# Three of four blocks of private activations move, in plain fp32, into the retrieval loop

## The chip, the cores and the metric

The kernel runs on one core of one Trainium2 chip. The metric is the device time of one execution in microseconds (us). Three runs of the kernel before gave 2097.33 us as their median (2095.89 to 2100.11). One execution was profiled; it took 2096.1 us, and its trace spans 2094.3 us from the first to the last instruction. All rows below are of that execution.

## What is computed

The reference is a stack of two layers on 2048 tokens of 256 features: attention with decay, a mixture of experts, a selective scan, and last a retrieval feed-forward; a layernorm follows each. The change is in the retrieval:

```python
h = silu(hidden_states @ W_up.T + b_up)          # 256 -> 1024
h = h @ W_down.T + b_down                        # 1024 -> 128, the "private activations"
q = h @ W_q.T                                    # 2 x 8 heads x 64
sim = einsum('pbthn,hkpn->pbthk', q, keys)       # 45 keys a head
scores, idx = top_k(sim, 8)
# best 8 of the 64 sums of each head -> indices into 2048 experts
z = silu(einsum('btd,bthkd->bthk', h, down_embed[indices]) * softmax(sc))
out = einsum('bthk,bthkd->btd', z, up_embed[indices])
```

## The kernel before, in words

The tokens are cut into 16 tiles of 128 (`TILES`) and 4 blocks of 512 (`BLK`, `NBLK`). `M.xT` holds the features of all tokens transposed, `h` the private activations of all tokens (128 features x 2048 tokens), `wk` the product of `W_q` and `keys`.

**`private_phase`** (from L1444) is a stage of its own. SyncE issues six loads (wu, bu, wd, bd, wq, keys) and then the retrieval's tables. TensorE waits for all six, forms `wk` (L1488) and then runs a loop over the 4 blocks. Each matrix is kept as a high part and a rest, both in fp32r, and a product is three fp32r matmuls: high by high, high by rest, rest by high. For a block these are 8 steps m (`UPT`) with 6 matmuls of 512 columns (L1500 to L1502), and 8 with 3 (L1510 to L1512). ScalarE applies Silu (L1563), VectorE splits the result into its two parts (L1544, L1546) and adds the bias (L1549). GpSimd splits the weights. A barrier of all engines ends the stage.

**`retrieval_phase`** (from L1573) then runs a software pipeline written out by hand, with semaphores and fixed orders of instructions on each engine. Its loop counter I goes from -3 to 16. In the pass I with all tiles alive, TensorE does, in this order: `gather(I)` (L1738, 192 small matmuls), the first quarter of `product(I-1)` (L1779), `select(I)` (L1751), then `fill_z(I+1)` (L1694) and `lower_z` (L1701) with the other quarters of `product(I-1)` and `turn(I+1)` (L1720, L1725) between them, `scatter(I)` (L1761), `scores(I+3)` (L1710) and `flip(I)` (L1771). VectorE does `marks(I)` (L1931, which `gather` needs; then L1922 and L1915), `normalize(I+1)`, `top_eights(I+2)` (L1975), `weigh(I)` (L1944 to L1949, needs `select`), `places_of(I+2)` (L1981, L1984), `cut(I)` (L1954 to L1966, needs ScalarE's `silu(I)`; `scatter` needs it), `bests` and `look_up(I+2)`, `add_out(I-1)`. ScalarE does the copies out of PSUM that lie between these (`pull` L1825, `copy_z` L1852, `copy_turned` L1844, `lift` L1831, `copy_scores` L1860, `copy_W` L1837), `silu(I)` (L1872) and, last in its pass, `soften(I+2)` (L1865, Exp). SyncE sends the tile's indices through DRAM and spreads them to all partitions, 2 MB (L1680). Passes -3 to -1 fill the pipeline; the first `gather` is in pass 0. A wait of the form `after(engine, name, count)` holds the engine until the semaphore has that count; what is behind it on the engine stays behind.

The PSUM banks `misc0` and `misc1` serve scores and z in turn; `ps_turned` serves `turn`. The buffers `W` and `masked` of the retrieval lie in the memory of `M.xT`, which nobody reads by then; `of_b` has two sets, used by alternate tiles.

## Time and profile before

| what | value |
|---|---|
| median of three runs | 2097.33 us |
| the profiled execution | 2096.1 us, span 2094.3 us |
| TensorE busy | 1773.3 us (85% of the span) |
| VectorE busy | 1275.2 us (61%) |
| ScalarE busy | 885.2 us (42%) |
| GpSimd busy | 487.4 us (23%) |
| mean granted TensorE clock | 0.939 of full |
| stage of the private activations | 1455.3 to 1553.0 us of the span |
| retrieval, pass -3 to the last sum | 1553.3 to 2077.3 us |

Busy shares are averages over stages with different limits, so the rows below are taken from the two stages that the change touches. A row of the timeline is: start, length, engine, line, operation, what it writes<-what it reads, how many instructions are merged; in brackets the idle time before it and what ended it. A merged row's length runs from the first start to the last end; matmuls are pipelined, so the spacing of starts is shorter than the length of one.

### The profile page before, as it was taken

To read this page: it belongs to the slowest core of one execution; us is meant where nothing else is said; L and a number is where in the kernel's file an instruction comes from. 1 tells how busy PE (TensorE), PEld (TensorE's weight loads), DVE (VectorE), ACT (ScalarE), POOL (GpSimd) and SP (SyncE) were. 2 spreads that over 40 slices of the span, in tenths; PEclk is the share of its full clock that TensorE was granted. 3 is DMA by queue.
4 is the path that set the end of the run, shared out by engine and by line. 5 is a ranking of instruction groups with operands and counts; after the bars stand their busy time and mean duration, and the time that the engine had idled before them with its cause. 6 is when DMAs were issued, how large, how long until landed. Compare 5 with 4: busy or idle time off the path is not lost. (4 is left out here: it accounts for less than half of the span.)

```text
span 2094.3 us, 44740 instructions
## 1 busy us (share of the span) xinstructions
PE 1773.3 (85%) x16696; PEld 1384.5 (66%) x16696; DVE 1275.2 (61%) x3096; ACT 885.2 (42%) x1542; POOL 487.4 (23%) x460
## 2 busy tenths in 40 slices
PE   6999999999997967999996466665977898989896
PEld 5888888888885756777773122222756787777775
DVE  0034344443445564644444799997369998989885
ACT  4533333333333332444444554443334655655652
POOL 1323342343326006600000466561200000000000
PEclk9999999999998976999998698888898999999998
DMA  2000000000002005223230000001103122122121
GB/s 85 18 2 23 23 23 10 13 23 23 23 10 93 0 9 176 91 86 88 82 99 23 0 0 1 0 0 50 66 0 123 43 83 84 43 83 84 43 83 42
DMA packets 55494, 96.81 MB, mean 46 GB/s; under 512 B 11424, under 2 KB 38176, under 8 KB 52776
## 3 DMA queue, kind: packets, MB, share of 16 engines
q1 hardware_dynamic: 55260, 94.94, 13.6%
q8 instruction: 84, 1.38, 0.3%
q14 instruction: 42, 0.34, 0.1%
q10 hardware_dynamic: 108, 0.15, 0.0%
HBM read 92.56 MB, written 2.51 MB: 45 GB/s over the span
## 5 line engine op out<-in xcount | busy, mean ns | idle before, releaser
L1351 POOL TENSOR_TENSOR sc_sb_bx<-sc_sb_dtx,sc_sb_bs 128x1024 f32<-128x1024 f32 x64 | 150.7, 2355 | 83.8 <-DVE sc_sb_h L1363 71.2
L1363 DVE TENSOR_TENSOR_SCAN sc_sb_h<-sc_ps_a,sc_sb_bx 128x512 f32<-128x512 f32 x128 | 150.5, 1209 | 20.6 <-ACT sc_ps_a L1341 20.6
L1852 ACT ACTIVATE re_sb_z<-re_ps_misc 128x512 bf16<-128x512 f32 x192 | 105.8, 594 | 124.0 <-PE re_ps_misc L1694 81.4
L544 POOL TENSOR_TENSOR g_sb_squares_sum<-g_sb_squares_sum,at_sb_qT 128x512 f32<-128x512 f32 x64 | 81.7, 1277 | 310.5 <-ACT at_sb_qT L475 310.5
L1067 DVE TENSOR_TENSOR mo_sb_gated<-mo_sb_hidden,mo_sb_gate 128x512 f32<-128x512 f32 x100 | 72.5, 725 | 131.2 <-ACT mo_sb_hidden L1037 130.7
L1037 ACT ACTIVATE mo_sb_hidden<-mo_ps_h,mo_sb_b 128x512 f32<-128x512 f32 x100 | 68.8, 688 | 162.3 <-PE mo_ps_h L995 162.0
L1284 PE MATMUL sc_ps_y<-sc_sb_hc,all_sb_ident 128*128 128x512 f32 x256 | 126.7, 626 | 0.0
L1779 PE MATMUL re_ps_out<-re_sb_up,all_sb_xT 128*128 128x256 f32 x512 | 121.9, 383 | 0.9 <-ACT all_sb_xT L1837 0.9
L506 DVE COPY at_sb_state<-at_ps_state_sum 128x128 f32<-128x128 f32 x64 | 18.6, 290 | 168.9 <-PE at_ps_state_sum L420 168.9
L1738 PE MATMUL re_ps_wheel<-re_sb_is_b,re_sb_z 128*32 128x128 bf16 x3072 | 76.4, 261 | 36.1 <-issue 30.2
L515 DVE SCALAR_TENSOR_TENSOR g_sb_gated<-at_ps_out,at_sb_nw,g_sb_gated 128x512 f32 x64 | 48.1, 751 | 94.3 <-ACT at_sb_qT L475 94.3
L1779 PEld LDWEIGHTS re_ps_out<-re_sb_up,all_sb_xT 128*128 128x128 f32 x512 | 95.0, 190 | 15.1 <-ACT all_sb_xT L1837 1.1
L1738 PEld LDWEIGHTS re_ps_wheel<-re_sb_is_b,re_sb_z 128*32 128x32 bf16 x3072 | 72.7, 192 | 41.3 <-issue 41.2
L475 ACT ACTIVATE at_sb_qT<-at_ps_out 128x512 f32<-128x512 f32 x64 | 38.2, 597 | 127.5 <-PE at_ps_out L436 127.5
L1275 PE MATMUL sc_ps_c<-sc_sb_bc_parts,sc_sb_state_rows 96*128 96x512 bf16 x64 | 27.2, 425 | 76.4 <-DVE sc_sb_hc L1371 76.4
L1329 ACT ACTIVATE sc_sb_bs<-sc_ps_b 128x512 f32<-128x512 f32 x64 | 38.1, 596 | 121.1 <-PE sc_ps_b L1275 121.1
L1005 PE MATMUL mo_ps_acc<-mo_sb_gatedH,mo_sb_w2H 128*128 128x512 f32 x200 | 81.4, 407 | 8.3 <-DVE mo_sb_gatedL L1059 8.3
L993 PE MATMUL mo_ps_h<-mo_sb_xH,mo_sb_w1H 128*128 x200 | 80.5, 402 | 6.0 <-DVE all_sb_xT_part L1054 6.0
L500 DVE TENSOR_TENSOR at_sb_weights<-at_ps_score,at_sb_tbl 128x512 f32<-128x512 f32 x128 | 81.9, 682 | 5.1 <-PE at_ps_score L407 5.1
L1230 POOL TENSOR_TENSOR sc_sb_dtx<-sc_sb_dt,all_sb_xT x8 | 12.7, 1582 | 307.3 <-DVE sc_sb_dt L1221 307.3
L1275 PEld LDWEIGHTS sc_ps_c<-sc_sb_bc_parts,sc_sb_state_rows 96*128 96x128 bf16 x64 | 6.2, 97 | 117.7 <-DVE sc_sb_hc L1371 116.7
L1341 ACT ACTIVATE sc_ps_a<-sc_sb_dt,sc_sb_decay 128x512 f32<-128x512 f32 x128 | 82.9, 685 | 1.8 <-DVE sc_sb_h L1363 1.8
(258 smaller groups left out, 5048.7 us busy)
## 6 DMA issues: line engine op xcount, KB each, us to landing
re_sb_b_all<-re_b SPq DMA_DIRECT2D x16, 2048.0 KB, 8.2
mo_sb_gate<-mo_gates SPq DMA_DIRECT2D x36, 256.0 KB, 3.1
mo_sb_w<-in_w_dram SPq DMA_DIRECT2D x10, 640.0 KB, 9.5
at_sb_w<-in_qkv_w_dram SPq DMA_DIRECT2D x18, 256.0 KB, 3.0
mo_sb_gate<-mo_gates SPq DMA_DIRECT2D x20, 192.0 KB, 2.7
mo_sb_gate<-mo_gates SPq DMA_DIRECT2D x16, 224.0 KB, 3.1
at_sb_tbl<-in_decay_dram SPq DMA_DIRECT2D x18, 193.5 KB, 2.3
mo_sb_gate<-mo_gates SPq DMA_DIRECT2D x20, 160.0 KB, 2.6
```

The source lines that it names most:

```text
L500: nc.vector.tensor_tensor(weights[:, h, :].rearrange("p (t q) -> p t q", t=CHUNKS), ps_score[h][:, :].rearrange("p (t q) -> p t q", t=CHUNKS),
L544: nc.gpsimd.tensor_tensor(part, part, qT[n][:, :], ALU.add).then_inc(summed, 1)
L993: nc.tensor.matmul(ps_h[f % NP][:, :], w1H[:, c, fs], xH[xs], start=(c == 0), stop=False)
L1005: nc.tensor.matmul(acc[d][:, :], w2H[:, g, of], gatedH[g % NH][:, :], start=(g == 0), stop=False)
L1067: nc.vector.tensor_tensor(gated[f % 2][:, :], hidden[f % 2][:, :], gate[f % NG][:, :], ALU.mult).then_inc(gated_ready, 1)
L1284: last = nc.tensor.matmul(ps_y[:, d * BLK:(d + 1) * BLK], M.ident[:, :], hc[g % HCS][:, d, :], start=(n == 0), stop=(n == STATES - 1))
L1341: nc.scalar.activation(a[g % 2][d][:, :], dt[:, d, tokens(g)], ACT.Exp, scale=decay[:, d, g % STATES:g % STATES + 1]).then_inc(a_ready, 1)
L1351: nc.gpsimd.tensor_tensor(bx[g % BXS][:, :, :], dtx[:, :, tokens(g)], bs[g % BSS][:, :].unsqueeze(1).broadcast_to([P, KD, BLK]), ALU.mult) ...
L1363: nc.vector.tensor_tensor_scan(h[g % 2][:, d, :], a[g % 2][d][:, :], bx[g % BXS][:, d, :], 0.0, ALU.mult, ALU.add).then_inc(scanned, 1)
L1738: last = nc.tensor.matmul(wheel[g * 2 * ROWS:(g + 1) * 2 * ROWS, j * P:(j + 1) * P], z[:, n, :, :, token].rearrange("p a r -> p (a r)"), i ...
L1779: last = nc.tensor.matmul(ps_out[:, 0:DM], W[:, a, :], up[:, a, :], start=(a == 0), stop=(a == ROWS - 1))
L1852: nc.scalar.activation(z[:, n, :, 4 * j:4 * j + 4, :], misc[j % 2][:, :].rearrange("p (r a t) -> p a r t", r=4, a=2), ACT.Copy).then_inc(S ...
```

## The change

`private_phase` keeps one block, the first (tokens 0 to 511), done in plain fp32: 2 matmuls a step for `wu`, 1 for `wd`, no splitting, nothing on VectorE or GpSimd. ScalarE also adds the bias. `wq` and `keys` are loaded first and waited for on their own. The other three blocks are 12 pieces of a quarter block of hidden units each (2 of the 8 steps m). Piece p belongs to block 1 + p // 4. In the retrieval's loop TensorE does `rise_product(I+3)` last in a pass and `private_product(I+2)` after `gather(I)`; ScalarE does `rise_up(I+3)` between `copy_W` and `soften`; VectorE does `keep_h(I+2)` between `top_eights` and `weigh`, which adds the piece into `h`. So pieces 0 to 11 go up in passes -3 to 8 and down in passes -2 to 9. New waits on `h_kept`, `up_ready`, `h_used` guard the shared banks. As `M.xT` is still read, `W` and `masked` get memory of their own, and `of_b` has one set in place of two, with a wait for the scatter of the tile before in `marks`.

```diff
 @block.tensor   (private_phase)
-                pe.wait_ge(loaded, 6 * 16)
+                pe.wait_ge(keys_loaded, 2 * 16)
...
-                with pe.Fori(0, NBLK) as i:
-                    pe.wait_ge(x_low, i + 1)
-                    for m in range(UPT + LAG):
...
+                pe.wait_ge(up_loaded, 4 * 16)
+                for m in range(UPT + LAG):
+                    if m < UPT:
+                        if m >= NB:
+                            pe.wait_ge(up_ready, m - NB + 1)
+                        for c in range(KD):
+                            last = nc.tensor.matmul(ps_up[m % NB][:, :], wu[:, c, m * P:(m + 1) * P],
+                                                    M.xT[:, c, 0:BLK], start=(c == 0), stop=(c == KD - 1))
+                        last.then_inc(up_product, 1)
+                    if m >= LAG:
+                        g = m - LAG
+                        pe.wait_ge(up_ready, g + 1)
+                        nc.tensor.matmul(ps_h[:, :], wd[:, g, :], rise[g % NB][:, :], start=(g == 0),
+                                         stop=(g == UPT - 1)).then_inc(h_product, 1)
...
+                act.wait_ge(h_product, UPT)
+                nc.scalar.activation(h[:, 0:BLK], ps_h[:, :], ACT.Identity, bias=bd[:, 0:1])
...
-        of_b = [[s.sb(f"of_b{n}{c}", [P, HALF_TWIN // 2, GRID, 2], BF16) for c in range(2)] for n in range(2)]
+        of_b = [s.sb(f"of_b{c}", [P, HALF_TWIN // 2, GRID, 2], BF16) for c in range(2)]
...
                 def scores(T, m):
+                    after(pe, "h_kept", T // 4 * 4)
...
                 def turn(T):
                     after(pe, "turned_ready", T * 2)
+                    after(pe, "h_kept", min(T + 2, PIECES))
...
+                def rise_product(piece, I):
+                    block = 1 + piece // 4
+                    for n in range(2):
+                        m = piece % 4 * 2 + n
+                        after(pe, "sim_ready", (I + 3) * 2 + n + 1)
+                        for c in range(KD):
+                            last = nc.tensor.matmul(misc[n][:, :], wu[:, c, m * P:(m + 1) * P],
+                                                    M.xT[:, c, block * BLK:(block + 1) * BLK],
+                                                    start=(c == 0), stop=(c == KD - 1))
+                        last.then_inc(S["up_product"], 1)
+
+                def private_product(piece, I):
+                    after(pe, "up_ready", 2 * (piece + 1))
+                    after(pe, "turned_ready", (I + 1) * 2)
+                    after(pe, "h_kept", piece)
+                    for n in range(2):
+                        last = nc.tensor.matmul(ps_turned[:, :], wd[:, piece % 4 * 2 + n, :], rise[n][:, :],
+                                                start=(n == 0), stop=(n == 1))
+                    last.then_inc(S["h_used"], 1)
...
                         for q in range(QUARTERS):
                             gather(I, q)
+                    if 0 <= I + 2 < PIECES:
+                        private_product(I + 2, I)
                     if live(I - 1):
                         product(I - 1, 0)
...
                             flip(I, q)
+                    if 0 <= I + 3 < PIECES:
+                        rise_product(I + 3, I)
...
+                def rise_up(piece):
+                    after(act, "h_used", piece)
+                    for n in range(2):
+                        after(act, "up_product", 2 * piece + n + 1)
+                        m = piece % 4 * 2 + n
+                        nc.scalar.activation(rise[n][:, :], misc[n][:, :], ACT.Silu, bias=bu[:, m:m + 1]
+                                             ).then_inc(S["up_ready"], 1)
...
                             copy_W(I, q)
+                    if 0 <= I + 3 < PIECES:
+                        rise_up(I + 3)
                     if live(I + 2):
                         soften(I + 2)
...
-                    after(dve, "scattered", (T - 1) * QUARTERS)
+                    after(dve, "scattered", T * QUARTERS)
                     of_bs(T, 0)
...
+                def keep_h(piece):
+                    after(dve, "h_used", piece + 1)
+                    after(dve, "h_kept", piece)
+                    of = h[:, (1 + piece // 4) * BLK:(2 + piece // 4) * BLK]
+                    if piece % 4 == 0:
+                        last = nc.vector.tensor_scalar(of, ps_turned[:, :], bd[:, 0:1], None, ALU.add)
+                    else:
+                        last = nc.vector.tensor_tensor(of, ps_turned[:, :], of, ALU.add)
+                    last.then_inc(S["h_kept"], 1)
...
                         top_eights(I + 2)
+                    if 0 <= I + 2 < PIECES:
+                        keep_h(I + 2)
                     if live(I):
                         weigh(I)
```

## Rows read from the trace of the kernel before

**Rows 1.** Stage windows: busy us of each engine, granted clock, DMA share, GB/s.
```profile
1455.00:1475.00 20.00, 8.36 (x35) 8.06 (x36) 4.63 (x4) 3.96 (x5) 8.35 (x20) 0.55 0.96 291
1831.00:1862.00 31.00, 28.28 (x548) 24.17 (x548) 28.55 (x110) 17.96 (x34) 0.00 (x0) 1.00 0.18 70
```

**Rows 2.** Timeline of TensorE, one pass of the retrieval (I = 3) and the next start.
```profile
1675.40 4.45 PE L1738 MATMUL re_ps_wheel<-re_sb_is_b,re_sb_z 128*32 128x128 bf16 x192 [1.71 <-issue]
...
1681.70 2.09 PE L1751 MATMUL re_ps_wheel<-re_sb_twin,re_sb_pulled 128*64 128x64 f32 x64
...
1701.81 1.91 PE L1771 MATMUL re_ps_wheel<-all_sb_ident,re_sb_lifted 128*128 128x128 f32 x16
1705.44 0.78 PE L1738 MATMUL re_ps_wheel<-re_sb_is_b,re_sb_z 128*32 128x128 bf16 x25 [1.72 <-issue]
```

**Rows 3.** Timeline of VectorE in the same pass.
```profile
1674.55 2.74 DVE L1931 TENSOR_SCALAR re_sb_is_b<-re_sb_b_all,re_sb_own 128x2048 bf16<-128x2048 bf16 x4
...
1684.55 1.27 DVE L1944 TENSOR_TENSOR all_sb_xT<-re_ps_wheel,re_sb_of_a 128x512 f32<-128x512 f32 x2
...
1692.21 0.23 DVE L1954 TENSOR_TENSOR re_sb_c_rest<-re_sb_c_whole,re_sb_c_parts 128x64 f32<-128x64 f32 x1 [0.62 <-ACT re_sb_c_parts L1874]
```

**Rows 4.** Timeline of ScalarE at the end of the same pass.
```profile
1704.59 1.28 ACT L1865 ACT_TABLE_LOAD   x1
1705.88 0.27 ACT L1865 ACTIVATE re_sb_soft<-re_sb_soft 128x64 f32<-128x64 f32 x1
```

**Rows 5.** Timeline of TensorE: the private stage's start, its end, and the fill.
```profile
1466.64 7.06 PE L1488 MATMUL pv_ps_k<-pv_sb_keys,pv_sb_wq 64*128 64x45 f32 x32 [12.25 <-DMA pv_sb_keys<-in_keys_dram]
1473.62 0.79 PE L1500 MATMUL pv_ps_up<-pv_sb_xH,pv_sb_wuH 128*128 x1
...
1477.49 0.40 PE L1500 MATMUL pv_ps_up<-pv_sb_xH,pv_sb_wuH 128*128 x1
1477.73 0.39 PE L1501 MATMUL pv_ps_up<-all_sb_xT_part,pv_sb_wuH 128*128 x1
...
1553.27 2.88 PE L1710 MATMUL re_ps_misc<-re_sb_wk,re_sb_h 128*128 128x360 f32 x8 [1.32 <-PEq L1474]
1561.70 3.78 PE L1694 MATMUL re_ps_misc<-re_sb_h,re_sb_down 128*128 128x128 f32 x16 [5.55 <-ACT re_sb_sim L1860]
...
1583.78 4.88 PE L1738 MATMUL re_ps_wheel<-re_sb_is_b,re_sb_z 128*32 128x128 bf16 x192 [5.54 <-DVE re_sb_is_b L1931]
```

**Rows 6.** Timeline; two source lines (ns min/median/max, first and last start); a DMA issue.
```profile
1435.15 5.32 PE L1284 MATMUL sc_ps_y<-sc_sb_hc,all_sb_ident 128*128 128x512 f32 x12
L1563 ACT ACTIVATE pv_sb_up<-pv_ps_up,pv_sb_bu x32: 681/688/689, 1477.9 to 1548.8; 128x512 f32<-128x512 f32 x32
L1549 DVE TENSOR_SCALAR re_sb_h<-pv_ps_h,pv_sb_bd x4: 751/751/752, 1495.3 to 1552.2; 128x512 f32 x4
pv_sb_wu<-in_w_up_dram SPq DMA_DIRECT2D x1, 1024.0 KB, 4.9
```

**Rows 7.** Timeline of VectorE in the fill, and clock windows there (columns of Rows 1).
```profile
1556.48 1.74 DVE L1975 MAX8 re_sb_top<-re_sb_sim 128x8 f32<-128x45 f32 x16
...
1582.89 2.74 DVE L1931 TENSOR_SCALAR re_sb_is_b<-re_sb_b_all,re_sb_own 128x2048 bf16<-128x2048 bf16 x4
1562.00:1565.00 3.00, 3.00 (x15) 3.00 (x15) 2.93 (x26) 2.15 (x4) 0.00 (x0) 0.50 0.01 3
```

**Rows 8.** Timelines: VectorE's marks of passes 1 and 14, TensorE's gather of pass 6.
```profile
1611.92 2.74 DVE L1931 TENSOR_SCALAR re_sb_is_b<-re_sb_b_all,re_sb_own 128x2048 bf16<-128x2048 bf16 x4
...
1768.54 2.26 PE L1738 MATMUL re_ps_wheel<-re_sb_is_b,re_sb_z 128*32 128x128 bf16 x92 [1.49 <-issue]
1772.04 2.50 PE L1738 MATMUL re_ps_wheel<-re_sb_is_b,re_sb_z 128*32 128x128 bf16 x100 [1.24 <-issue]
...
2018.62 2.74 DVE L1931 TENSOR_SCALAR re_sb_is_b<-re_sb_b_all,re_sb_own 128x2048 bf16<-128x2048 bf16 x4
```

More of the change, by code:

```diff
@@ L1459, in private_phase @@
         NB, LAG = 4, 2
-        up = [s.sb(f"up{n}", [P, BLK]) for n in range(NB)]
-        upH = [s.sb(f"upH{n}", [P, BLK], FP32R) for n in range(NB)]
-        upL = [s.sb(f"upL{n}", [P, BLK], FP32R) for n in range(NB)]
+        rise = [s.sb(f"rise{n}", [P, BLK]) for n in range(NB)]
         ps_up = [s.ps(f"up{n}") for n in range(NB)]
@@ L1568, in _ @@
                                          ps_k[n][:, 0:RHEADS * KEYS], ACT.Copy)
+                act.wait_ge(up_loaded, 4 * 16)
+                for m in range(UPT):
+                    act.wait_ge(up_product, m + 1)
+                    if m >= NB:
+                        act.wait_ge(h_product, m - NB + 1)
+                    nc.scalar.activation(rise[m % NB][:, :], ps_up[m % NB][:, :], ACT.Silu,
+                                         bias=bu[:, m:m + 1]).then_inc(up_ready, 1)
+                act.wait_ge(h_product, UPT)
+                nc.scalar.activation(h[:, 0:BLK], ps_h[:, :], ACT.Identity, bias=bd[:, 0:1])
 def retrieval_phase(nc, M, D):
@@ L1598, in load_tables @@
                 sp.dma_start(to, of).then_inc(tables_loaded, 16)
-        private_phase(nc, M, D, h, wk, load_tables)
+        wu = s.sb("wu", [P, KD, CROSS])
+        wd = s.sb("wd", [P, UPT, PRIV])
+        bu = s.sb("bu", [P, UPT])
+        bd = s.sb("bd", [P, 1])
+        private_phase(nc, M, D, h, wk, wu, wd, bu, bd, load_tables)
+        rise = [s.sb(f"rise{n}", [P, BLK]) for n in range(2)]
+        PIECES = (NBLK - 1) * UPT // 2
         sim = s.sb("sim", [P, 2 * RHEADS, KEYS])
```

108 lines of the change are left out of this document (17 added, 91 removed).

## The prediction

> **What bounds the kernel now.** I read the windows by stage first, then the timelines of TensorE and VectorE over one pass of the retrieval, then both ends of the private stage, then the fill between the two.
>
> The private stage runs from the first load at 1455.3 us to 1553.3, where the first scores start [rows 5]. The first eleven microseconds go to loads: TensorE waits for the last of six, `keys`, until 1466.64. Then 7.06 us go to `wk` at about half clock (0.55 in that window, rows 1), and the four blocks run from 1473.62. At full clock an fp32r matmul of 512 columns starts 0.24 us after the one before (1477.49 and 1477.73, rows 5). A block has 8 x 6 + 8 x 3 = 72 of them, and TensorE sets the pace: (1553.3 - 1473.6) / 4 = 19.9 us a block, waits at its ends and the barrier included.
>
> In the retrieval TensorE and VectorE bound the pass together. In pass 3, `gather` starts at 1675.40 and again at 1705.44: 30.04 us [rows 2]. TensorE's only long rest is ahead of `gather`: `flip` ends at 1701.81 + 1.91 = 1703.72, then 1.72 us idle. It waits there for VectorE: the marks start at 1674.55 and the first quarter takes a quarter of 2.74 us, then `gather` goes [rows 3]. VectorE is busy nearly throughout and has one wait, 0.62 us for ScalarE's Silu of z at 1692.21, which comes through TensorE's `turn`. So the loop is closed this way: marks, gather, select, turn, Silu, `cut`, `look_up`, marks. TensorE's own work is 28.3 us of the pass. Other passes look the same; marks of pass 1 start at 1611.92 and of pass 14 at 2018.62 [rows 8], so the mean pass is 406.7 / 13 = 31.3 us. The excess over 30.0 sits in some passes in gaps inside `gather`, as the 1.24 us at 1772.04 [rows 8]. TensorE is busy 28.3 of 31 us at full clock [rows 1].
>
> **Unit prices.** A plain fp32 matmul appears as two instructions in the trace: `product` has 256 calls, `scores` 32 and the scores of one tile already count as four. Twelve instructions of 512 columns take 5.32 us [rows 6]; less the 0.59 us of the last one that is 0.43 us each, so 0.86 us a call. `rise_product` is 4 calls, 3.4 us; `private_product` 2 calls, 1.7 us; a piece 5.1 us, twelve pieces 62 us. Three blocks before cost 59.7 us. On TensorE alone the change saves nothing: what it can gain is the place. `rise_up` is two Silus of 0.69 us, `keep_h` one VectorE step of 0.75 us [rows 6].
>
> **The private stage after.** Removed: everything of three blocks, and the start that waits for all loads. `wq` and `keys` now go first. They have not been seen in that place. `wu`, twice as large, landed 4.9 us after its issue in first place [rows 6], so 1461 is my value for `keys`; the other end is 1466.6, as now. `wk` then takes 7.1 us, to 1468, and the other four loads are in by 1466.6. One block is 16 + 8 = 24 calls, 24 x 0.86 = 20.6 us at full clock. Now the clock became full some 10.8 us after TensorE started (1466.64 to 1477.5, rows 5); if that repeats, full clock comes at 1471.8 and the 3.6 us before are worth 1.8, so the block ends at 1490.6. ScalarE's bias (0.2 + 0.7) and the same 0.3 us to the first scores give 1491.8. Against 1553.3 that is **-61.5 us**; with `keys` late, -56.
>
> **The fill (passes -3 to -1).** Here VectorE bounds: busy from 1556.48 without a gap to the marks of tile 0 at 1582.89 [rows 7], and TensorE waits 5.55 and 5.54 us [rows 5]. In the same coordinates: scores of tile 0 (the first half of the row at 1553.27) end at 1554.7, `rise_product(0)` runs behind them to 1558.1, its Silus end at 1559.0, `private_product(0)` at 1560.8. `top_eights(0)` ends at 1556.48 + 1.74 = 1558.2, and behind it VectorE now waits in `keep_h(0)` for that product: 2.8 us, and 0.75 for the step itself, so everything behind on VectorE is 3.5 us late. The scores of tile 1, whose copy waits for VectorE's `places_of`, come as late, and with them `rise_product(1)`, which stands ahead of `fill_z(0)` on TensorE. At full clock TensorE's chain of rise 1, Silu, down 1, z of tile 0, scores 2, rise 2 ends before VectorE is there, and the fill costs 3.5 + 0.75 = 4.3 us. But TensorE idles before it, and at just this place the clock now falls to half (0.50 at 1562 to 1565, after the rest of 5.55 us; rows 5, 7). At half clock `rise_product(1)` takes 6.8, down 1 3.4, and the chain (an estimate: about 14 us for z and scores 2, from 3.78 us for each of z's two fills at half clock and the copies between, and 3.4 for rise 2) ends 11 to 12 us later than `gather(0)` now starts. The rest ahead of it is shorter than now (some 3 us), so I take the middle, **+8 us**, range 4 to 12.
>
> A page speaks against this place: the Trainium skill (ScalarE: Activation LUTs, What ACT_TABLE_LOAD costs) prices a switch of table set at 2.66 us, a load of 1.28 and a drain of 1.38. The trace agrees on the load (1.28 us) but the Exp starts 0.01 us behind it [rows 4]. The new order Silu, Exp, Silu, Exp in the fill adds two switches, 2.6 us by the row and 5.3 by the page, both on ScalarE beside VectorE's 26 us.
>
> **The loop.** Pass 0 has no `product`, so TensorE has room: `keep_h` 0.75 and what of rise 3 sticks out past the marks, 3.4 - 1.8 = 1.6 us: +1.5 to 2.4, taken as **+2**. In passes 1 to 8 `private_product` stands between `gather` and `select`, and `rise_product` between `flip` and the next `gather`. TensorE's path from one `gather` to the next becomes 28.3 + 5.1 = 33.4 us. VectorE's: c_parts came 16.8 us after `gather` and comes 1.7 later, 18.5; from there to the next marks 12.4 and to `gather` 0.85 as now: 31.8 us. TensorE sets the pass: 33.4 against 30.0, +3.4 us. That is 5.1 less the 1.72 us of rest, which goes. Eight passes: **+27 us**. Pass 9 has only the down part: +1.7 on the path through `turn`: **+2 us**. Covered, and with what: `keep_h` (0.75) by VectorE's wait for `select`: `select` ends at 8.4 us after `gather` now (1681.70 + 2.09) and at 10.1 then, while VectorE, its marks 0.85 + 1.6 us ahead of `gather`, is there at -2.45 + 10.0 + 0.75 = 8.3; `rise_up` (1.4) by ScalarE, 18 us busy of 31, and it needs no new table, since `silu(I)` left Silu in place and only copies follow. `soften` behind it moves to 2.5 us after `gather` starts, so the first `pull` is about 1.3 us late; quarters come every 1.1 us and a copy takes 0.6, so the fourth is on time. If that cover failed it would cost up to 1.3 us a pass, 12 us in all. Queued behind `rise_product` is `gather`; behind `keep_h`, `weigh`. The single `of_b`: its wait for the scatter of the tile before is reached some 34 us after the `gather` of that tile's pass; the scatter is over before `flip`, which starts at 26.4 now (1701.81) and 28.1 then; nothing, and 6 us in hand. SyncE's queue is unchanged. Long passes: the gaps inside `gather` may stay or go, as the 2 MB spread now falls earlier against it; 0 to -9 us over eight passes (their excess over 30.0 in total), and I take 0.
>
> **Sum.** -61.5 + 8 + 2 + 27 + 2 = -22.5. On the profiled execution's own 2096.1 us that gives 2073.6; the median of the runs lies 1.2 above it. I say **2074.5 us**.
>
> **The rivals.**
> - *The gaps go too.* With the rest before `gather` gone TensorE never pauses, the excess of the long passes (9 us) vanishes and the fill stays at full clock (-4): 2061. For: some long passes have gaps marked as issue, not as waits. Against: nothing shows that they depend on VectorE.
> - *The cover fails in part.* `keys` land late (+5.5), the fill at half clock (+4) and the late `pull` (up to +12, half of it taken, +6): 2090. For: ScalarE's order is now pull behind soften behind Silu behind the rise. Against: the arithmetic above.
> - *The loop takes the additions in full (slower).* Mechanism: rise, Silu, down, keep and marks turn out to be one chain, so that the 1.7 us of rest is a wait for something behind the rise and is not filled. Then each of passes 0 to 8 costs 5.1 + 0.75 = 5.9 us, 53 in all, pass 9 2.5, the fill 12: +67.5 against -61.5, so 2103. It decides from 5.2 us a pass (12 + 9 x 5.2 + 2.5 = 61.3). For: every piece adds a semaphore round over three engines. Against: VectorE's marks need nothing of pass I's rise.
> - *No net change.* The same chain in part, just at that 5.2 us a pass: 2097.
>
> **How the numbers follow.** Forecast (2067 to 2082) 0.56; gaps go (2057 to 2067) 0.16; cover fails (2082 to 2093) 0.16; no net change 0.04; slower 0.08. About 0.2% (4 us) is what a measurement of this kernel can tell from no change. Faster: 0.56 + 0.16 + 0.16 = 0.88; same 0.04; slower 0.08. The range leaves out a tenth at either side: 2061 to 2089.
>
> **What would show it.** Right: the first scores some 61 us earlier; marks of pass 0 some 26 to 38 us behind them plus 3; a spacing of `gather` of 33.4 us in passes 1 to 8 and 30 to 31 from pass 10; no idle time ahead of `gather` in passes 1 to 8; VectorE's waits for `select` of 1 to 2 us. Wrong: idle time ahead of `gather` beside a longer pass (slower rival), a `pull` that holds up `select` (cover), or half clock in passes 1 to 8.

## The result

The changed kernel takes 2064.93 us (median of 4 runs, 2062.97 to 2070.13) against 2098.01 us for the kernel before (4 runs, 2095.89 to 2100.11). The ratio is 0.9843, 95% interval 0.9826 to 0.9861: 33 us faster. A second set of 5 runs of the same kernel gave 0.9849 [0.9832, 0.9865]. The time is below the forecast of 2074.5 us and inside the range of 2061 to 2089 us. It does not lie in the forecast's own band (2067 to 2082) but in that of the rival "the gaps go too" (2057 to 2067, chance 0.16). The profiled execution took 2062.97 us (span 2061.2) beside 2096.1 (span 2094.3) before.

I cut both executions at the same events, and the pieces add up to the whole difference of 33.1 us. "First scores" is the start of `scores` of tile 0, "gather(n)" the first gather of pass n.

| stretch | before | after | difference | forecast |
|---|---|---|---|---|
| start to first scores | 1553.27 | 1492.54 | -60.7 | -61.5 |
| first scores to gather(0) | 30.51 | 34.55 | +4.0 | +8 |
| pass 0 | 28.99 | 31.42 | +2.4 | +2 |
| passes 1 to 8 | 250.03 | 271.58 | +21.6 | +27 |
| pass 9 | 32.71 | 31.79 | -0.9 | +2 |
| passes 10 to 15 and the end | | | +0.5 | 0 |

The stretch up to the first scores, and then the fill, on the timeline of TensorE of the kernel after (they answer to [rows 5]; start, duration, engine, line, operation, output and inputs, count, in brackets the idle time before and what ended it):

```profile
1460.80 7.05 PE L1476 MATMUL pv_ps_k<-pv_sb_keys,pv_sb_wq 64*128 64x45 f32 x32 [6.72 <-DMA pv_sb_keys<-in_keys_dram]
1467.78 2.07 PE L1485 MATMUL pv_ps_up<-all_sb_xT,re_sb_wu 128*128 128x512 f32 x2
...
1492.54 1.45 PE L1656 MATMUL re_ps_misc<-re_sb_wk,re_sb_h 128*128 128x360 f32 x4 [1.02 <-PEq L1462]
1493.95 3.70 PE L1738 MATMUL re_ps_misc<-all_sb_xT,re_sb_wu 128*128 128x512 f32 x8
1498.42 1.98 PE L1749 MATMUL re_ps_turned<-re_sb_rise,re_sb_wd 128*128 128x512 f32 x4 [0.78 <-ACT re_sb_rise L1855]
...
1504.56 5.26 PE L1738 MATMUL re_ps_misc<-all_sb_xT,re_sb_wu 128*128 128x512 f32 x8 [2.94 <-ACT re_sb_sim L1833]
...
1527.09 1.16 PE L1685 MATMUL re_ps_wheel<-re_sb_is_b,re_sb_z 128*32 128x128 bf16 x41 [0.81 <-DVE re_sb_is_b L1915]
```

`keys` are there at 1460.80 instead of 1466.64, `wk` takes as long as before, the block starts at 1467.78. In the fill the timeline of VectorE shows the new wait in `keep_h(0)`, and the marks of tile 0, which answer to [rows 7]:

```profile
1500.45 0.75 DVE L2038 TENSOR_SCALAR re_sb_h<-re_ps_turned,re_sb_bd 128x512 f32<-128x512 f32 x1 [2.96 <-PE re_ps_turned L1749]
...
1526.20 2.74 DVE L1915 TENSOR_SCALAR re_sb_is_b<-re_sb_b_all,re_sb_own 128x2048 bf16<-128x2048 bf16 x4
```

`gather(0)` waits 0.81 us for those marks: VectorE, not TensorE, sets the end of the fill.

One pass of the loop on TensorE (pass 2, answering to [rows 2]). The two added pieces are L1749 and L1738:

```profile
1592.27 4.57 PE L1685 MATMUL re_ps_wheel<-re_sb_is_b,re_sb_z 128*32 128x128 bf16 x192
1596.77 1.98 PE L1749 MATMUL re_ps_turned<-re_sb_rise,re_sb_wd 128*128 128x512 f32 x4
...
1600.41 2.09 PE L1698 MATMUL re_ps_wheel<-re_sb_twin,re_sb_pulled 128*64 128x64 f32 x64
...
1620.47 1.91 PE L1718 MATMUL re_ps_wheel<-all_sb_ident,re_sb_lifted 128*128 128x128 f32 x16
1622.22 3.60 PE L1738 MATMUL re_ps_misc<-all_sb_xT,re_sb_wu 128*128 128x512 f32 x8
1625.75 0.50 PE L1685 MATMUL re_ps_wheel<-re_sb_is_b,re_sb_z 128*32 128x128 bf16 x11
```

From gather to gather it is 33.48 us, and no idle time stands in brackets ahead of the second gather, where [rows 2] had 1.72 us. `rise_product` ends where `gather` starts. The window of that pass, with the columns of [rows 1]: TensorE is busy 32.30 of 33 us at full clock, where it was 28.28 of 31.

```profile
1592.00:1625.00 33.00, 32.30 (x560) 26.05 (x560) 29.02 (x110) 19.31 (x35) 0.00 (x0) 1.00 0.18 66
```

VectorE in the same pass on its timeline (answering to [rows 3]), and after it ScalarE on its own:

```profile
1599.76 0.73 DVE L2038 TENSOR_SCALAR re_sb_h<-re_ps_turned,re_sb_bd 128x512 f32<-128x512 f32 x1
1601.68 0.69 DVE L1928 TENSOR_TENSOR re_sb_masked<-re_ps_wheel,re_sb_of_a 128x512 f32<-128x512 f32 x1 [1.19 <-PE re_ps_wheel L1698]
...
1610.91 0.22 DVE L1938 TENSOR_TENSOR re_sb_c_rest<-re_sb_c_whole,re_sb_c_parts 128x64 f32<-128x64 f32 x1 [1.91 <-ACT re_sb_c_parts L1847]
```

```profile
1596.89 0.60 ACT L1798 ACTIVATE re_sb_pulled<-re_ps_wheel 128x512 f32<-128x512 f32 x1 [0.41 <-PE re_ps_wheel L1685]
```

VectorE now has 1.19 and 1.91 us to spare (0.62 in [rows 3]), and the fourth `pull` ends at 1597.5, well before `select` at 1600.41: both covers of the forecast hold.

One pass is not like the others. In pass 5 the matmuls of `gather` stop for 3.07 us, marked as issue, and the next gather is at 1729.45, 36.65 us after this one (1692.80):

```profile
1692.80 4.47 PE L1685 MATMUL re_ps_wheel<-re_sb_is_b,re_sb_z 128*32 128x128 bf16 x190
1700.35 0.28 PE L1685 MATMUL re_ps_wheel<-re_sb_is_b,re_sb_z 128*32 128x128 bf16 x2 [3.07 <-issue]
...
1729.45 1.80 PE L1685 MATMUL re_ps_wheel<-re_sb_is_b,re_sb_z 128*32 128x128 bf16 x68
```

I call the time of passes 1 to 8 above eight undisturbed ones the *excess*: before 250.03 - 8 x 30.04 = 9.7 us, after 271.58 - 8 x 33.4 = 4.4 us. This is where the time went better than forecast, beside the fill, and most of the experiments are about it. Each excess below is that of one profiled execution. The base is a regular pass near the shortest of its kernel; what the other passes without a visible gap take above it (mostly under 0.6 us each) counts in the excess too.

### The profile page after: what moved, and what is told of

Its sections match the earlier page's. It is cut to its first block and busy times, and to the rows that moved or that the text cites. A ratio compares the mean times of both kernels' runs of the same rounds, so it can differ in the third digit from the quotient of the medians.

```text
span 2061.2 us, 44242 instructions
## 1 busy us (share of the span) xinstructions
PE 1782.8 (86%) x16600; PEld 1361.4 (66%) x16600; DVE 1240.5 (60%) x3036; ACT 879.3 (43%) x1538; POOL 475.1 (23%) x428
## 3 DMA queue, kind: packets, MB, share of 16 engines
q8 instruction: 85, 1.39, 0.3%
## 5 line engine op out<-in xcount | busy, mean ns | idle before, releaser
L1726 PE MATMUL re_ps_out<-re_sb_up,re_sb_W 128*128 128x256 f32 x512 | 121.0, 381 | 0.9 <-ACT re_sb_W L1810 0.9
L1726 PEld LDWEIGHTS re_ps_out<-re_sb_up,re_sb_W 128*128 128x128 f32 x512 | 95.7, 190 | 18.6 <-issue 4.5
```

Source lines behind the costliest of these rows:

```text
L1726: last = nc.tensor.matmul(ps_out[:, 0:DM], W[:, a, :], up[:, a, :], start=(a == 0), stop=(a == ROWS - 1))
```

## The experiments

Each ratio is against the kernel before in the same set of runs (medians 2096.4 to 2098.5 us).

**Is it the place, or the cheaper arithmetic?** The loop of the kernel before, with the private stage doing all four blocks in plain fp32 and `wq` and `keys` loaded first:

```diff
-                                nc.tensor.matmul(ps_up[m % NB][:, :], wuH[:, c, of], xH[xs], start=(c == 0), stop=False)
-                                nc.tensor.matmul(ps_up[m % NB][:, :], wuH[:, c, of], xL[xs], start=False, stop=False)
-                                last = nc.tensor.matmul(ps_up[m % NB][:, :], wuL[:, c, of], xH[xs],
-                                                        start=False, stop=(c == KD - 1))
...
+                            last = nc.tensor.matmul(ps_up[g % NB][:, :], wu[:, c, m * P:(m + 1) * P],
+                                                    M.xT[:, c, i * BLK:(i + 1) * BLK], start=(c == 0), stop=(c == KD - 1))
```

> The kernel before with one part of the change: the private stage as in the change (wq and keys loaded first, plain fp32, no splitting), but for all four blocks, and the retrieval's loop untouched. Theory of place: the gain of the change comes from where the three blocks are done, not from how. The stage then starts its first block 6 us earlier (1467.8 for 1473.6), a block takes 8 x 2.57 = 20.6 us for 19.9, the end 0.9: first scores at about 1467.8 + 1.8 + 82.4 + 1.2 = 1553 us of the span, as before; the time within 3 us of before. Rival, the cheaper stage: the stage without splits and with earlier loads carries a third or more of the 33 us; then 11 us or more faster than before.

Measured: 2094.78 us (10 runs), ratio 0.9988 [0.9978, 0.9997]. The timeline of TensorE:

```profile
1463.05 7.05 PE L1480 MATMUL pv_ps_k<-pv_sb_keys,pv_sb_wq 64*128 64x45 f32 x32 [6.90 <-DMA pv_sb_keys<-in_keys_dram]
...
1556.50 1.97 PE L1661 MATMUL re_ps_misc<-re_sb_wk,re_sb_h 128*128 128x360 f32 x5 [1.02 <-PEq L1466]
```

From `wk` to the first scores it is 93.4 us, against 86.6 in [rows 5]: the plain work is 6.8 us longer. It gets 5.3 us of that back by its start: `wk` begins 6.0 us after the first load is issued, where it was 11.3. From the first load to the first scores the stage takes 99.4 us against 98.0. By the medians the kernel is 2.5 us faster, within the 3 us expected. So a stage of its own costs nearly the same in either arithmetic, and the 33 us come of the place. The opposite half, the old arithmetic in the new place, was not run.

**What does the rest ahead of gather take in?** The kernel before with unused fp32 matmuls behind `flip` in passes 1 to 8, two (1.7 us a pass) and four (3.4 us); the edit with four:

```diff
+                    if 1 <= I <= 8:
+                        after(pe, "sim_ready", (I + 3) * 2 + 2)
+                        for n in range(4):
+                            nc.tensor.matmul(misc[n % 2][:, :], down[:, 0:P], down[:, P:P + BLK], start=True, stop=True)
```

> The kernel before with two plain fp32 matmuls of 512 columns (1.7 us of TensorE, on the tables, into the banks that rise_product uses) behind flip in passes 1 to 8; they are used by nobody. Theory: the 1.7 us of rest ahead of gather is a wait for VectorE's marks and takes them in full: 0 us in all (0 to +2), gather to gather still 30 to 33 us. Rival, one chain: the rest moves behind them, 8 x 1.7 = +14 us.

> The same with four such matmuls, 3.4 us, the whole of a rise_product. Theory: 1.7 us of each is taken by the rest, 1.7 sticks out: 8 x 1.7 = +14 us (+11 to +16), no rest left ahead of gather; less if the gaps inside gather get rarer once the 2 MB spread starts ahead of it. Rival, one chain: +27 us.

Measured: with two 2093.74 us, ratio 0.9986 [0.9975, 0.9996]; with four 2114.94 us, 1.0085 [1.0068, 1.0102]. The timeline of TensorE with two, one pass:

```profile
1706.24 1.88 PE L1822 MATMUL re_ps_misc<-re_sb_down 128*128 128x512 f32 x4
1708.20 1.03 PE L1738 MATMUL re_ps_wheel<-re_sb_is_b,re_sb_z 128*32 128x128 bf16 x36
```

Passes 1 to 8 take 249.9 us as before (250.0): the rest of 1.72 us is filled free of charge. The next 1.7 us have their full price: 264.5, or 14.6 us more for 8 x 1.7 = 13.8. By the medians the four cost 17.7 us over the kernel before, more than the 11 to 16 expected. The profiled execution with four was the shortest of its runs and the one with two among their longest, so the step between these two is less certain than its decimals. It is still the forecast's step "5.1 less the 1.72 us of rest", and it rules out the slower rival, in which the rest can't be filled. But the rest is gone here too and the excess stayed: 9.6 with two, 10.3 with four (over an undisturbed pass of 31.77). So taking the rest away isn't enough to lower the excess, as the rival "the gaps go too" had it.

**Do the gaps belong to the 2 MB spread?** The spread of the slot numbers over the partitions (`b_all`) cut from 2 MB to 16 KB from tile 1 on, in the kernel before and in the kernel after. The output is then not that of these tokens, since the marks compare old slot numbers; every instruction of the engines stays.

```diff
-                    sp.dma_start(b_all[:, :, :].rearrange("p t k -> p (t k)"), b_dram[T % 2].partition_broadcast(P)
-                                 ).then_inc(S["b_spread"], 16)
+                    if T:
+                        sp.dma_start(b_all[:, 0, 0:SLOTS], b_dram[T % 2][0:SLOTS].partition_broadcast(P)
+                                     ).then_inc(S["b_spread"], 16)
...
```

> The kernel before with the spread of the indices cut from 2 MB to 16 KB from tile 1 on (so the marks and the output of tiles 1 to 15 are not those of their tokens; all instructions but that DMA are the same). Theory: the gaps inside gather and select, marked issue, come when TensorE's instruction stream has to be refilled while the 2 MB spread fills the DMA engines. Without it they go, every pass 1 to 13 is 30.0 us, and the kernel is 13 to 17 us faster. Rival, the gaps have nothing to do with the DMAs: the same passes (2, 5, 6, 8, 9, 12) stay 1 to 3 us long, within 3 us of before.

> The changed kernel with the spread cut to 16 KB from tile 1 on (marks and output of tiles 1 to 15 are then not those of their tokens). Cutting it took 9 us off the kernel before, and the gaps in select went while part of those in gather stayed. Theory: the changed kernel has already got rid of some of what the spread costs, since the spread now starts 1.7 us ahead of gather and runs beside rise_product; so less is left, 3 to 6 us. Rival, the lower cost of passes 1 to 8 has another cause: again 9 us.

Measured: on the kernel before 2088.22 us, ratio 0.9959 [0.9945, 0.9973], 9 us less; on the kernel after 2060.02 us, 0.9821 [0.9805, 0.9838], 6 us less than its second set of runs (2066.03). Passes 1 to 8 fall to 245.1 (excess 4.8) and to 268.8 (excess 1.6). The expectation for the kernel before, 13 to 17 us, was too high. In the kernel after, the gap of pass 5 shrinks from 3.07 to 0.42 us at the same matmul, the last two of 192; in the kernel before, gaps inside gather remain up to 1.35 us (the 1.61 in the rows below is the rest ahead of it). The timelines of TensorE, first of the kernel after with the small spread, then of the kernel before with it:

```profile
1691.78 4.50 PE L1689 MATMUL re_ps_wheel<-re_sb_is_b,re_sb_z 128*32 128x128 bf16 x190
1696.70 0.28 PE L1689 MATMUL re_ps_wheel<-re_sb_is_b,re_sb_z 128*32 128x128 bf16 x2 [0.42 <-issue]
```

```profile
1860.09 2.47 PE L1742 MATMUL re_ps_wheel<-re_sb_is_b,re_sb_z 128*32 128x128 bf16 x103 [1.61 <-issue]
1863.92 2.23 PE L1742 MATMUL re_ps_wheel<-re_sb_is_b,re_sb_z 128*32 128x128 bf16 x89 [1.35 <-issue]
```

So the transfer makes the long gaps long, but something of TensorE's own instruction supply is there without it.

**Can the spread be made gentler?** The kernel after with the spread in four parts of 512 KB, each issued when the one before has landed:

```diff
+                    for n in range(4):
+                        of = slice(n * P * SLOTS // 4, (n + 1) * P * SLOTS // 4)
+                        sp.dma_start(b_all[:, :, :].rearrange("p t k -> p (t k)")[:, of],
+                                     b_dram[T % 2][of].partition_broadcast(P)).then_inc(S["b_spread"], 16)
+                        sp.wait_ge(S["b_spread"], (T * 4 + n + 1) * 16)
```

> The changed kernel with the 2 MB spread issued as four parts of 512 KB, each after the one before has landed; all of it is done, over some 14 us of the pass in place of 10, and it is needed only 20 us later. Theory: the long gaps on TensorE (3.07 us in pass 5, and 1 to 1.6 in passes 11 and 12) come when a refill of its instruction stream has to pass a long spread; shorter bursts shorten them: 3 to 6 us faster than the changed kernel. Rival, the gaps are the refill's own or the spread's total: within 2 us of it.

Measured: 2066.12 us, ratio 0.9848: no gain, where 3 to 6 us were expected. Passes 1 to 8 take 272.1 us; pass 5 is 35.4 us long with its gap shortened to 1.79, and pass 3, regular before, is 35.8 with one of 2.13. So in these passes nothing is gained. But the total hides two changes that cancel. Beside the second set's profiled execution the fill is 3.8 us longer (38.35 for 34.57), because the four parts in series bring the indices of tile 0 later and `gather(0)` waits 4.65 us for the marks, and passes 10 to the end are 2.8 us shorter (197.3 for 200.1). Whether smaller parts help where the fill doesn't pay for them stays open.

**The kernel after once more, and without the wait in keep_h(0).** The second set of runs of the unchanged kernel after, and one edit that puts `keep_h(0)` behind VectorE's `places_of` of its pass:

```diff
-                    if 0 <= I + 2 < PIECES:
+                    if 0 <= I + 2 < PIECES and I > -2:
                         keep_h(I + 2)
...
+                    if I == -2:
+                        keep_h(I + 2)
```

> The changed kernel once more, unchanged, as the yardstick on this chip for the three beside it: 2063 to 2070 us.

> The changed kernel with keep_h(0) of pass -2 moved behind places_of(0) on VectorE; all else as it is. Theory: the fill costs 4 us because VectorE waits 2.96 us in keep_h(0) for private_product(0), ahead of places_of(0), on which the scores of tile 1 and rise 1 hang; with the step behind places_of that wait is covered, TensorE does not idle and rise 1 runs at full clock (3.6 us for 5.26): marks of tile 0 some 3 us earlier, 3 us faster than the changed kernel. Rival, TensorE's chain through rise 1, down 1, z and rise 2 bounds the fill: 0 to 1 us.

Measured: unchanged 2066.03 us (2063.16 to 2069.54), edited 2064.46 us (2058.8 to 2065.81), ratios 0.9849 and 0.983. The fill behaves as calculated: from the first scores to the marks of tile 0 it is 30.61 us instead of 33.66. On TensorE the rest ahead of the second rise is gone and the rise has its full speed:

```profile
1504.31 3.70 PE L1738 MATMUL re_ps_misc<-all_sb_xT,re_sb_wu 128*128 128x512 f32 x8
...
1700.64 0.28 PE L1685 MATMUL re_ps_wheel<-re_sb_is_b,re_sb_z 128*32 128x128 bf16 x2 [2.94 <-issue]
```

But passes 1 to 8 take 274.4 us instead of 271.6: pass 5 is again long (38.4 us, the last row), and pass 3 as well (35.1, with a gap of 1.58). The gap of pass 5 is no longer than before; its pass is 1.7 us longer because the granted clock fell behind the gap, and `private_product` took 3.41 us for 1.98:

```profile
1700.86 3.41 PE L1749 MATMUL re_ps_turned<-re_sb_rise,re_sb_wd 128*128 128x512 f32 x4
```

```profile
1701.00:1705.00 4.00, 4.00 (x7) 1.99 (x8) 0.69 (x1) 0.56 (x1) 0.00 (x0) 0.57 0.02 4
```

In the kernel after the clock stayed at 1.00 from 1700.5 to 1705 us, behind a gap of 3.07. The repeated run of the unchanged kernel has its one long pass at the same place, pass 5 with 36.4 us and a gap of 2.77. In all of them the gap of pass 5 stands behind the 190th matmul of `gather`. The one of pass 3 is new here, and stands at the same matmul (behind the 169th) as in the kernel with the spread in parts. So an edit on VectorE leaves the places as they are and changes which of them show a gap.

**TensorE's whole added work, on the kernel before.** The run with four matmuls behind `flip`, and two more (1.7 us) between gather and the first select:

```diff
+                    if 1 <= I <= 8:
+                        after(pe, "turned_ready", (I + 1) * 2)
+                        for n in range(2):
+                            nc.tensor.matmul(ps_turned[:, :], down[:, 0:P], down[:, P:P + BLK], start=True, stop=True)
```

> The kernel before with TensorE's whole added work of passes 1 to 8 and nothing else of the change: four unused plain fp32 matmuls (3.4 us) behind flip and two (1.7 us) between gather and the first select. Compare with the run that has the first four alone: 2114.9, passes 1 to 8 264.5 us, of which 10.5 are long passes. Theory (the gaps lie in what TensorE does beside the 2 MB spread, and the change moves select and the following product out from beside it): the passes take 33.4 us plus less than 5 us of excess in all, 267 to 272 us, and the time is 2118 to 2123. Rival (the excess stays whatever stands there; the change loses it for another reason): 8 x 33.4 + 10 = 277 us and 2128 to 2130.

Measured: 2121.22 us (4 runs, 2119.66 to 2125.78), ratio 1.0114 [1.0097, 1.0131]. The time is the theory's, but the profiled execution, the longest of the four, is the rival's: passes 1 to 8 take 277.3 us, six of them 33.3 to 34.0, two of them 38.19 and 37.51. It is 4.6 us above the median. Part of that may lie ahead of the retrieval, where this kernel equals the one before: `wk` starts 3.6 us later than in that one's profiled execution. The timeline of TensorE in the first of these:

```profile
1684.02 4.33 PE L1738 MATMUL re_ps_wheel<-re_sb_is_b,re_sb_z 128*32 128x128 bf16 x184
1691.25 0.39 PE L1738 MATMUL re_ps_wheel<-re_sb_is_b,re_sb_z 128*32 128x128 bf16 x8 [2.89 <-issue]
```

Two things follow. The undisturbed pass of 33.4 us is TensorE's added work and nothing else of the change (no ScalarE or VectorE step of it is in this kernel). And "the work moves out from beside the spread" didn't by itself bring the smaller excess: the same placing of work has 10.1 us of it in this execution. Some 3 us of that are the clock: behind the gaps of 2.89 and 2.52 us it fell to 0.58 and 0.57 (means of 4 us). The three shorter executions were not profiled, so this is one case, not a mean.

**Only the place in TensorE's instruction stream.** The kernel after with 96, then with 32, semaphore increments on TensorE ahead of its wait for `keys`; no work is changed:

```diff
+                for n in range(32):
+                    pe.sem_inc(pad, 1)
                 pe.wait_ge(keys_loaded, 2 * 16)
```

> The kernel after with 96 semaphore increments on TensorE ahead of its wait for keys, where it has nothing to do: no work is changed, every later instruction of TensorE lies 96 places further on in its stream. Theory (the one long pass, the fifth, with its 2.8 to 3.1 us gap at 7.5 us in gather, is where a refill of TensorE's instructions meets the spread): the long pass is another one, or its gap another size, and the time is 2062 to 2070. Rival (the gap belongs to pass 5's own data or addresses): pass 5 is again 36.4 to 36.7 us long and every other one 33.4 to 33.8.

> The kernel after with 32 instead of 96 semaphore increments on TensorE ahead of its wait for keys. The 96 took 15.6 us there (0.163 us each) where only some 6.7 were idle and so held up wk by themselves; 32 take 5.2 us and fit into the 6.72 us of waiting: first scores again at 1492.4 to 1492.8 us, and only the place of every later instruction in TensorE's stream is changed. Theory (the gaps are where TensorE's instructions are fetched beside the 2 MB spread, so they go by the place in the stream): other passes than the fifth are long, by 1 to 5 us each, and the time is 2063 to 2075. Rival (the three long passes with the 96 come of the later start): with the start as before only the fifth pass is long, at 36.4 to 36.7 us, and the time is 2063 to 2069.

Measured: with 96 2080.08 us, ratio 0.9918 [0.9904, 0.9933]; with 32 2070.91 us, 0.9866 [0.9849, 0.9882]. The 96 were a badly chosen size: TensorE was idle for 15.6 us ahead of `wk`, which started at 1471.91, and the first scores came at 1502.60, 10.1 us late by the increments' own cost. That is most of the miss against the expected 2062 to 2070; the other part is more gaps. The 32 hide as intended. The timeline of TensorE with 32:

```profile
1461.66 7.05 PE L1478 MATMUL pv_ps_k<-pv_sb_keys,pv_sb_wq 64*128 64x45 f32 x32 [7.76 <-DMA pv_sb_keys<-in_keys_dram]
...
1492.88 1.45 PE L1658 MATMUL re_ps_misc<-re_sb_wk,re_sb_h 128*128 128x360 f32 x4 [1.02 <-PEq L1462]
...
1701.43 0.65 PE L1687 MATMUL re_ps_wheel<-re_sb_is_b,re_sb_z 128*32 128x128 bf16 x18 [3.07 <-issue]
...
1773.48 1.02 PE L1751 MATMUL re_ps_turned<-re_sb_rise,re_sb_wd 128*128 128x512 f32 x2 [1.73 <-issue]
```

The first scores are 0.3 us from where they were, and yet the kernel is 5 us slower than in its second set of runs. Pass 5 is still the longest, now 38.55 us (1.7 of it again half clock behind the gap, 0.57 from 1702 to 1706) and with its gap at another matmul (18 before the end of gather, not 2); pass 7 is long as well, with a gap inside `private_product`, and of the later passes the 12th takes 35.42 us (33.32 in the kernel after). The excess of passes 1 to 8 is 7.8 us. With 96 the long passes are 2, 4 and 9 (37.21, 34.99, 36.39 us) and pass 5 is regular at 33.46. That pass 5's own data or addresses make the gap is ruled out: with 96 increments it has none, and with 32 it has it elsewhere. The expectation that with 32 pass 5 would be regular was wrong.

The shift itself can be read off. With 32 increments the gap of pass 5 comes 16 matmuls earlier (174 for 190), those of pass 12 16 earlier (89 for 105, 216 for 232), and the one of pass 11 15 earlier (130 for 145); with 96 the last is 47 earlier (98). Each of these matmuls has a weight load of its own, so 16 of them are 32 instructions and 48 are 96. The possible places of a gap are fixed in TensorE's stream; which of them show one is not, as the edit on VectorE showed.

The profile page of the kernel after has, in its part on DMA queues, TensorE's own instruction queue:

```profile
q8 instruction: 85, 1.39, 0.3%
```

85 packets with 1.39 MB are 16 KB each, and three of them fall into the 20 us from 1685 to 1705, in which pass 5 has its gap. The Trainium skill (Runtime: NRT & Kernel Launch, Instruction fetch mechanics) says that an engine's instructions come in blocks of 16 KiB by a DMA queue of its own, and that this fetch is mostly hidden. The trace agrees on the size. On the second point it agrees for most of the packets, but some of the fetches show. The DMA view of the kernel after for the gap of pass 5 alone, from 1697.2 to 1700.4 us, has one such packet among those of the spread (queue q1):

```profile
q1 hardware_dynamic: 67, 0.85, 63.8%
q8 instruction: 1, 0.02, 1.9%
```

In the trace this packet starts at 1697.94 and ends at 1698.90, and the matmuls go on at 1700.35, 1.45 us later. It is the same in the other kernels. From the first to the last `gather` the fourteen kept traces have 98 gaps of more than 0.35 us marked issue that are not at the first matmul of a gather. Every one of them ends 1.2 to 1.6 us after a packet of this queue has ended. The 100 idle times of that size ahead of the first matmul of a gather are different: there the last packet had ended at least 2.9 us before. So those, the rests for the marks, are not of this kind. The 98 are waits for the next block of instructions. They run from 0.4 to 3.1 us and get shorter when the 2 MB transfer is cut. What stays open is which block comes late: that I could not work out.

**A version with both small things mended.** The kernel after with `keep_h(0)` later, the loads of `wu`, `bu`, `wd`, `bd` ahead of `wq` and `keys`, and `wk` formed inside the first block, at full clock:

```diff
+                    if m == 5:
+                        pe.wait_ge(keys_loaded, 2 * 16)
+                        for n in range(2 * RHEADS):
+                            last = nc.tensor.matmul(ps_k[n // RHEADS][:, n % RHEADS * KEYS:(n % RHEADS + 1) * KEYS],
+                                                    wq[:, n, :], keys[:, n, :], start=True, stop=True)
+                        last.then_inc(k_product, 1)
...
```

> The kernel after with two edits: keep_h(0) behind places_of of its pass (alone: 2064.5, the fill 3.05 us shorter), and the loads of wu, bu, wd and bd ahead of wq and keys, with wk formed between the tiles 4 and 5 of the first block's up products, at full clock. Theory: wk takes some 4 us there instead of 7.05 at half clock, the blocks start when wu has landed (about 1460.8), and the half clock falls on up products instead: first scores 0 to 3 us earlier than 1492.5, time 2059 to 2065. Rival: the wait for keys (up to 1466.6) now falls inside the block, or the full clock comes later after it: no gain or a loss of up to 3 us.

Measured: 2062.44 us (2059.36 to 2063.04), ratio 0.9833 [0.9819, 0.9848]. The timeline of TensorE, then windows (busy of each engine, then the granted clock, third number from the right):

```profile
1462.29 7.34 PE L1486 MATMUL pv_ps_up<-all_sb_xT,re_sb_wu 128*128 128x512 f32 x12 [8.77 <-DMA re_sb_bd<-in_b_down_dram]
...
1475.58 3.77 PE L1479 MATMUL pv_ps_k<-pv_sb_keys,pv_sb_wq 64*128 64x45 f32 x32
1479.27 3.23 PE L1486 MATMUL pv_ps_up<-all_sb_xT,re_sb_wu 128*128 128x512 f32 x4
1482.31 1.51 PE L1492 MATMUL pv_ps_h<-pv_sb_rise,re_sb_wd 128*128 128x512 f32 x2
```

```profile
1475.00:1479.00 4.00, 4.00 (x33) 3.42 (x31) 0.00 (x0) 0.51 (x1) 0.00 (x0) 1.00 0.00 1
1479.00:1482.00 3.00, 3.00 (x8) 1.46 (x7) 0.00 (x0) 0.00 (x0) 0.00 (x0) 0.64 0.00 0
```

`wk` takes 3.77 instead of 7.05 us, as expected. But behind its 32 matmuls of 45 columns the granted clock falls, though TensorE was busy throughout, and the next six instructions take 4.4 us (1479.27 to 1483.65) instead of 2.6. The first scores come at 1491.70, 0.8 us earlier than in the kernel after, though TensorE started 1.5 us later: 2.3 us were gained, of some 3. The fill is again 3.05 us shorter. Of these 4 us passes 1 to 8 take back most (passes 3 and 5 with 35.71 and 38.23 us, excess 8.1), 1.7 us of it by half clock behind the gap of pass 5 (0.57 from 1698 to 1702). It is the fastest version of all that compute the whole, 2.5 to 3.6 us below the two sets of runs of the changed kernel, but the intervals overlap.

## Why the forecast was right, and where it was off

*The private stage, -61.5: right, -60.7.* `keys` were there at 1460.80 (value taken: 1461), `wk` kept its 7.05 us, the first up product was at 1467.78 (1468). The late end of the range (1466.6) didn't come. The 0.7 us too few are the clock: the first twelve instructions of the block took 8.29 us where 5.3 would be full speed, 3.0 us lost against the 1.8 taken.

*The fill, +8: over-sized; it was +4.0.* The wait in `keep_h(0)` was 2.96 us (2.8) and the step 0.75. The step that failed is the middle taken between full and half clock for TensorE's chain. The granted clock did fall, and `rise_product(1)` took 5.26 us, between 3.6 and 6.8; but the matmuls behind it ran at full clock again (down 1 in 1.98 us), so the chain stayed hidden behind VectorE and only the full-clock figure of 4.3 counted. The windows of the kernel after:

```profile
1501.00:1505.00 4.00, 1.06 (x4) 0.49 (x3) 3.97 (x37) 0.83 (x2) 0.00 (x0) 0.92 0.00 0
1505.00:1510.00 5.00, 4.82 (x8) 1.64 (x7) 4.83 (x30) 0.83 (x2) 0.00 (x0) 0.73 0.00 0
```

The rest ahead of that rise was 2.94 us instead of 5.55 [rows 5], as foreseen, and that shorter rest should have moved the value towards the lower end, not to the middle. The extra switches of table cost what [rows 4] showed. On ScalarE's timeline of the kernel after the load takes 1.28 us and Exp follows 0.01 us after it:

```profile
1510.57 1.28 ACT L1838 ACT_TABLE_LOAD   x1
1511.86 0.26 ACT L1838 ACTIVATE re_sb_soft<-re_sb_soft 128x64 f32<-128x64 f32 x1
```

The Trainium skill (ScalarE: Activation LUTs, What ACT_TABLE_LOAD costs) adds to each switch a drain of 1.38 us. It does not show here.

*Pass 0, +2: right, +2.4.*

*Passes 1 to 8, +27: the mechanism right, the size 5.4 too large.* The undisturbed pass is 33.4 us (33.40 to 33.76 in seven of eight), no idle time is ahead of gather, VectorE waits for `select` 1 to 2 us, and `keep_h`, `rise_up` and the later `pull` are covered. The fillers show the same by themselves: 1.7 us free, the rest at full price. The step that failed is "0 to -9 us ..., and I take 0": the excess fell from 9.7 to 4.4 us, 5.3 less, by two things.

About 2.1 us is the clock. The prediction put the excess down to gaps inside gather and took the passes to be at full clock, by the window of pass 8 alone. But in passes 2 and 5 of the kernel before the granted clock fell at the start of `gather`, and `gather` took 5.41 and 5.63 us where [rows 2] had 4.45. The timeline of TensorE, and the window of the first:

```profile
1643.07 5.41 PE L1738 MATMUL re_ps_wheel<-re_sb_is_b,re_sb_z 128*32 128x128 bf16 x192 [1.80 <-issue]
...
1735.65 5.63 PE L1738 MATMUL re_ps_wheel<-re_sb_is_b,re_sb_z 128*32 128x128 bf16 x192 [2.00 <-issue]
```

```profile
1643.00:1648.00 5.00, 4.81 (x180) 4.59 (x184) 5.00 (x6) 2.52 (x5) 0.00 (x0) 0.66 0.46 164
```

Both stand behind the rest that the change fills, so in this part the rival "the gaps go too" was right that TensorE's rest costs. It did not cost it every time: behind rests of 1.83 and 1.80 us in passes 1 and 7 the clock stayed at 1.00. In passes 1 to 8 of the kernel after, and of its second profiled execution, it is 1.00 throughout. There was luck in that too: behind gaps of about 3 us it fell in the kernels with `keep_h(0)` later, with 32 increments and with `wk` inside, and cost 1.7 us each.

Of the other 3.2 us, 1.3 are waits for instructions: those over 0.35 us come to 4.4 us in passes 1 to 8 before and to 3.1 after. The remaining 1.9 us I can't assign, and why the waits got fewer is open. The reason that the forecast gave, that the spread now lies earlier, is not borne out by the kernel before with all six matmuls: it has the same placing and, in the one execution profiled, 10.1 us of excess. Over the profiled executions of six kernels or sets of runs with the change's loop and the full, undivided spread the excess is 4.4, 4.6, 5.9, 7.2, 7.8 and 8.1 us, mean 6.3; over five with the loop of before, with or without fillers, it is 7.8, 9.6, 9.7, 10.1 and 10.3, mean 9.5. This looks as if some 3 us went with the change's loop and some 2 with the luck of where this kernel's stream lies. It is not shown: each figure is one execution, the clock is in them, the two groups touch, and executions of one kernel lie up to 7 us apart (with two fillers 2091.16 to 2098.49). With the 32 increments these passes take 3.4 us more and the whole kernel 5 us.

*Pass 9, +2: right against a pass of 30.04 (31.79, so +1.75)*, but before's own pass 9 was a long one (32.71), which the sum left out; it came out as -0.9. The forecast had the mean pass of 31.3 at hand and took the short one.

*The single of_b: no wait for it shows anywhere.* In TensorE's list of waits from 1500 to 2060 us (what was waited for and what released it, total, times, longest) the scatters waited twice for VectorE, and the nine waits of gather are the gap of pass 5 and passes 10 to 15:

```profile
PE re_ps_wheel L1685 <- issue: 14.8, 9, 3.1
...
PE re_ps_wheel L1708 <- DVE re_sb_spread L1950: 2.0, 2, 1.1
```

VectorE's list has no entry for the step that writes `of_b`.

A kernel with two buffers of it was not tried, so this rests on the traces alone.

In short, the forecast was right by its large terms, the private stage and the pass of 33.4 us, and three smaller errors of one sign brought the time to the lower end of the range: -61.5 + 8 + 2 + 27 + 2 = -22.5 was forecast, -60.7 + 4.0 + 2.4 + 21.6 - 0.9 + 0.5 = -33.1 came. The difference of 10.6 us is the fill (4.0), the excess (5.4) and pass 9 (2.9), less 1.7 in the other terms.

## What to carry to other kernels

Work that costs the same wherever it runs still pays when it is moved: count the rest of the bounding engine in each pass (here 1.72 us, filled for nothing), charge the remainder in full, and set it against the stage that disappears. Before spending a gain of one or two tenths of a per cent on an edit, see whether the long passes moved: here an edit that saved 3.05 us in the fill brought 1.6 us by the medians, and in the profiled execution passes that it doesn't touch took 2.6 us more. And an undisturbed pass is the right base for a bounding engine's path, but a sum of differences needs the disturbed ones on both sides.

## What the runs showed of the hardware that was not expected

- Thirty-two semaphore increments fitted into a wait of 7.76 us, but with 96 of them TensorE was idle for 15.6 us, at most 0.16 us each: no free way to shift a stream.
- Gaps of 0.4 to 3.1 us marked as issue, inside runs of small matmuls. All 98 over 0.35 us in the loop end 1.2 to 1.6 us after a packet of 16 KB on the instruction queue. A 2 MB transfer beside them makes them longer (3.07 to 0.42 us when it was cut), and 32 increments that do no work, 240 us ahead, move them by 32 instructions.
- The granted clock fell from 1.00 to 0.64 (mean of 3 us, between the levels of 1.2 and 2.4 GHz) right behind 3.8 us of matmuls of 45 columns, without any rest of TensorE. It fell in passes 2 and 5 of the kernel before behind rests of 1.80 and 2.00 us, and behind the gap of 2.94 us with `keep_h(0)` later, but not behind the rest of 1.83 us in pass 1 or the gap of 3.07 us in the kernel after.
